# A gather order, a deferred up sum, a gate and a table load moved in the tail of a one-core Perceiver block

## The reference, cut to what matters

```python
x = x + xattn(_layernorm(x), ctx, ctx, w_q, w_k, w_v, w_o)      # 4 batches, 16 heads, 2048 keys
x = x + retention(_layernorm(x), W_Q, W_K, W_V, W_G, W_O, gn_weight, gn_bias)
    # ... Yn = (Y - mean) * rsqrt(var + EPS); out = G * sigmoid(G) * (Yn * gn_weight + gn_bias) @ W_O
x = x + fff_block(_layernorm(x), ...)

def _fff(x, nw, nb, w1, b1, w2, b2, act):       # used four times: q, k, v (relu) and f (gelu)
    node = 0
    for _ in range(8):
        logit = einsum('bsd,bsd->bs', x, nw[node]) + nb[node]
        node = 2 * node + 1 + (logit > 0)
    leaf = node - 255
    h = act(einsum('bsd,bsdl->bsl', x, w1[leaf]) + b1[leaf])    # 16 hidden values per token
    return einsum('bsl,bsld->bsd', h, w2[leaf]) + b2[leaf]

# fff_block: q, k, v = three trees of xn; y = xn + softmax(q k^T / sqrt(D)) v; return y + f(y)
```

## Time and profile before

| what | value |
|---|---|
| median of 3 runs | 668.21 us (666.90 to 668.83) |
| profiled execution, its own time | 667.87 us |
| its span, first to last instruction | 666.0 us |
| granted TensorE clock, mean | 0.987 |
| busy share PE / DVE / ACT / Pool | 93% / 68% / 59% / 40% |
| the same in the tail alone, 586 to 666 us: PE, DVE, ACT, Pool | 71%, 50%, 32%, 43% |

### The profile page before, as it was taken

One profiled execution on the slowest core, in us unless ns is written; L12 is line 12 of the kernel. 1 busy time (PEld: TensorE's weight loads), 2 busy tenths in 40 slices (PEclk: granted clock), 3 DMA queues, 4 the chain that ended last, 5 costly groups with the idle time before them and its releaser, 6 DMA issues.

```text
span 666.0 us, 10952 instructions
## 1 busy us (share of the span) xinstructions
PE 617.3 (93%) x4214; PEld 537.9 (81%) x4217; DVE 452.2 (68%) x800; ACT 391.7 (59%) x834; POOL 269.5 (40%) x259
## 2 busy tenths in 40 slices
PE   8899999999999999898999999899999999887486
PEld 4688888999998989787989889678989898774475
DVE  2566656778766777776777776786777777754644
ACT  3765556576655555668564855867556855730254
POOL 3210001131111106895252347886161439845632
PEclk9999999999999999999999999999999999998599
DMA  9810000020100007140030027120120035203903
GB/s 200 226 34 1 1 0 1 1 64 19 47 1 1 1 1 274 52 131 0 1 132 1 1 76 317 38 95 1 25 108 1 1 107 223 67 2 131 386 7 138
DMA packets 21403, 48.54 MB, mean 73 GB/s; under 512 B 1509, under 2 KB 14697, under 8 KB 17257
## 3 DMA queue, kind: packets, MB, share of 16 engines
q0 software_dynamic: 4608, 34.74, 13.9%
q1 hardware_dynamic: 16168, 12.85, 7.2%
q10 hardware_dynamic: 576, 0.26, 0.1%
HBM read 47.59 MB, written 0.26 MB: 72 GB/s over the span
## 4 chain that ended last, share of the span: by engine, by line
PE 64%; POOL 12%; DVE 10%; ACT 6%; DMA 3%; SPq 2%; issue 2%; POOLq 0%; DVEq 0%; ACTq 0%
PE ps_s L442 22%; PE ps_av L442 20%; PE ps_ring L710 13%; POOL leaf L1502 4%; PE ps_ring L442 4%; PE ps_m L442 4%; DVE pt_lo L1133 2%; POOL leaf L1506 2%; DVE chunk_max L1353 2%; ACT prob L1048 2%; ACT pt_hi L979 2%; POOL ct_lo L1471 2%; DVE hid L1194 1%; DMA stage<-ctx_rows_dram 1%; DMA leaf<-down_f_dram,idx 1%
## 5 line engine op out<-in xcount | busy, mean ns | idle before, releaser
L979 ACT CAST pt_hi<-ps_ring 128x512 fp32r<-128x512 f32 x256 | 144.4, 590 | 147.2 <-PE ps_ring L710 146.9
L1133 DVE TENSOR_TENSOR pt_lo<-ps_ring,pt_hi 128x512 fp32r<-128x512 f32 x256 | 170.0, 686 | 65.3 <-ACT pt_hi L979 65.3
L1048 ACT ACTIVATE prob<-ps_s,neg_max 128x1024 f32<-128x1024 f32 x128 | 141.7, 1114 | 27.9 <-DVE neg_max L1436 27.7
L710 PE MATMUL ps_ring<-ident,prob 128*128 128x128 f32 x1024 | 145.0, 274 | 12.9 <-DVE q_lo L1133 4.9
L1353 DVE TENSOR_REDUCE chunk_max<-ps_s 128x1 f32<-128x1024 f32 x128 | 150.5, 1215 | 4.1 <-PE ps_s L442 3.9
L442 PE MATMUL ps_av<-pt_hi,c_hi 128*128 128x256 f32 x512 | 151.2, 295 | 0.0
L710 PEld LDWEIGHTS ps_ring<-ident,prob 128*128 128x128 f32 x1024 | 116.8, 140 | 40.1 <-issue 19.7
L442 PE MATMUL ps_av<-pt_lo,c_hi 128*128 128x256 f32 x512 | 144.7, 283 | 0.0
L442 PE MATMUL ps_av<-pt_hi,c_lo 128*128 128x256 f32 x512 | 144.6, 283 | 0.0
L442 PE MATMUL ps_s<-ct_hi,q_hi 128*128 128x512 f32 x256 | 112.6, 440 | 3.1 <-ACT prob L1048 2.4
L442 PE MATMUL ps_s<-ct_hi,q_lo 128*128 128x512 f32 x256 | 101.8, 398 | 0.0
(11 more groups left out here) (277 smaller groups left out, 754.1 us busy)
## 6 DMA issues: line engine op xcount, KB each, us to landing
stage<-ctx_t_dram SPq DMA_DIRECT2D x16, 256.0 KB, 3.1
stage<-ctx_rows_dram SPq DMA_DIRECT2D x16, 256.0 KB, 3.2
leaf<-w_v_dram SPq DMA_DIRECT2D x1, 512.0 KB, 7.8
leaf<-w_o_dram SPq DMA_DIRECT2D x1, 512.0 KB, 10.0
dec<-decay_dram SPq DMA_DIRECT2D x1, 512.0 KB
nw<-node_w_dram SPq DMA_DIRECT2D x1, 510.0 KB
wsm<-w_small_dram SPq DMA_DIRECT2D x1, 448.0 KB
leaf<-wq_t_dram SPq DMA_DIRECT2D x1, 384.0 KB, 10.9
```

The costliest lines, as they stand in the source:

```text
L710: last = nc.tensor.transpose(o[:, i * P:(i + 1) * P], prob[:, n % 2, k:k + P], ident[:])
L979: nc.scalar.copy(pt_hi[:, pp, row:row + KPC, P * (n % 2):P * (n % 2 + 1)], ps_ring[:, i % 2, :].rearrange("p (k q) -> p k q", k=KPC)).then ...
L1048: nc.scalar.activation(prob[:, n % 2, 1024 * e:1024 * (e + 1)], ps_s[:, 1024 * e:1024 * (e + 1)], ACT.Exp, bias=neg_max[:, n:n + 1], accum ...
L1133: return nc.vector.tensor_tensor(o, a, b_, op)
```

## The change

No arithmetic is added or removed but for seven idle products that become four ahead of `gated_t`, with three new ones ahead of the third batch's f tree. The rest is a different order or a different engine:

- Gathers of the last batch: up q, down q, up k, up v, down k, down v becomes up q, up k, down q, down k, up v, down v. Pool's `weigh0` and `up2` move behind `up1` and `weigh1`.
- The third batch's up sum on DVE moves from behind the last `pick_f` to behind the last batch's softmax scaling (place 68 of the last batch), and no longer waits for the last cast of leaf numbers.
- All 16 down blocks of the third batch's f tree go to ACT (12 before, 4 on DVE).
- The last batch's gate: Pool only forms the root and signals `group_root`; the product and the sum run on DVE, behind the third batch's `pick_f`.
- Both halves of the last batch's masked queries on DVE; before, the second was Pool's.
- The gelu table load on ACT moves from ahead of the `y_t` copies to behind them.
- The third batch's `attv` on PE moves behind the last batch's `score1`.

```diff
 BEFORE_LAST_AT = {
-    ... ("PE", "attv"): 77.5, ...
+    ... ("PE", "attv"): 79, ...
-    ... ("ACT", "gelu"): 106,
-    ("ACT", "down3"): 107,
+    ... ("ACT", "gelu"): 105,
+    ("ACT", "down3"): 106,
-    ... ("DVE", "hid3"): 107,
+    ... ("DVE", "hid3"): 100,
-    ("DVE", "own3"): 108,
+    ("DVE", "own3"): 1000,
 LAST_AT = {
+    ("DVE", "gate"): 51, ("Pool", "mask_q"): 1000,
-    ... ("Pool", "weigh0"): 58, ("Pool", "weigh1"): 62, ("Pool", "up2"): 60, ...
+    ... ("Pool", "weigh0"): 60, ("Pool", "weigh1"): 62, ("Pool", "up2"): 63, ...
-    ("ACT", "load_gelu"): 70,
+    ("ACT", "load_gelu"): 72,
-WARM = {("gated_t", B - 1): 7, ("xf_t", B - 1): 12}
+WARM = {("logits_f", B - 2): 2, ("path_f", B - 2): 1, ("gated_t", B - 1): 4, ("xf_t", B - 1): 12}
 def shares(b, t):
-    return (0, 12, 4) if (b, t) == (B - 2, 3) else (LW, LW // 2, 0)
+    return (0, LW, 0) if (b, t) == (B - 2, 3) else (LW, LW // 2, 0)
 def leaf_sum(t, pieces=None):
-                        pe.wait_ge(S["own_ready"], 2)
+                        pe.wait_ge(S["own_ready"], 1)
 def third_sum():
-                pe.wait_ge(S["own_ready"], 1)
-                for l in range(shares(B - 2, 3)[1], LW):
-                    mm(o, ident[:], rows[:, D * l:D * (l + 1)], False, False)
 def hidden_layer(b, t):
                     dve.wait_ge(S["got_up3"], 16 * (b + 1))
-                    dve.wait_ge(S["idx_ready"], 4 * B)
 # DVE, "rope" of the last batch
                         masked_queries(nc.vector, 0).then_inc(S["qmask_last"], 1)
+                        masked_queries(nc.vector, 1).then_inc(S["qmask_ready"], 1)
 # DVE, new step
+                elif k == "gate":
+                    bc = rstd[:].rearrange("p (h o) -> p h o", o=1).to_broadcast([P, RH, RE])
+                    dve.wait_ge(S["group_root"], 1)
+                    dve.wait_ge(S["scaled"], b + 1)
+                    link(tt(groups(gated), groups(yc), bc, ALU.mult))
+                    dve.wait_ge(S["silu_ready"], b + 1)
+                    tt(gated, gated, shift, ALU.add).then_inc(S["gated_ready"], 1)
 # Pool, "gate"
                     pool.wait_ge(S["var_ready"], variances(b, 1))
+                    if last:
+                        root(0, RH, var[:]).then_inc(S["group_root"], 1)
+                        return
 # Pool, "gather_up01" of the last batch
                     gather(b, 0)
-                    pool.wait_ge(S["ring_filled"], RING[("T", HEADS - 1, CH - 1)] + 1)
-                    pool.wait_ge(S["ring_free"], BY_DVE[("X", HEADS + 3, 0)])
-                    gather_down(b, 0)
                     pool.wait_ge(S["picked"], 4 * b + 3)
                     nc.gpsimd.tensor_copy(idx[:, 1:3], chosen[:, 1:3]).then_inc(S["idx_ready"], 2)
                     pool.wait_ge(S["idx_ready"], 4 * b + 3)
                     gather_up(b, 1)
+                    pool.wait_ge(S["ring_filled"], RING[("T", HEADS - 1, CH - 1)] + 1)
+                    pool.wait_ge(S["ring_free"], BY_DVE[("X", HEADS + 3, 0)])
+                    gather_down(b, 0)
+                    gather_down(b, 1)
                     gather_up(b, 2)
-                    gather_down(b, 1)
                     gather_down(b, 2)
```

More of the change, by code:

```diff
@@ L62 @@
 BEFORE_LAST_AT = {
-    ("PE", "qk_t"): 72, ("PE", "att"): 73.5, ("PE", "v_half"): 73, ("PE", "v_rest"): 76, ("PE", "attp_t"): 76, ("PE", "attv"): 77.5, ("PE", "y_t"): 80,
+    ("PE", "qk_t"): 72, ("PE", "att"): 73.5, ("PE", "v_half"): 73, ("PE", "v_rest"): 76, ("PE", "attp_t"): 76, ("PE", "attv"): 79, ("PE", "y_t"): 80,
     ("PE", "logits_f"): 81, ("PE", "path_f"): 82,
-    ("ACT", "qk_t"): 73, ("ACT", "att"): 76, ("ACT", "attp_t"): 77, ("ACT", "v_sum_copy"): 78, ("ACT", "y_t"): 81, ("ACT", "gelu"): 106,
-    ("ACT", "down3"): 107,
-    ("DVE", "attmax"): 75, ("DVE", "y"): 80, ("DVE", "turns_f"): 82, ("DVE", "pick_f"): 83, ("DVE", "hid3"): 107,
+    ("ACT", "qk_t"): 73, ("ACT", "att"): 76, ("ACT", "attp_t"): 77, ("ACT", "v_sum_copy"): 78, ("ACT", "y_t"): 81, ("ACT", "gelu"): 105,
+    ("ACT", "down3"): 106,
+    ("DVE", "attmax"): 75, ("DVE", "y"): 80, ("DVE", "turns_f"): 82, ("DVE", "pick_f"): 83, ("DVE", "hid3"): 100,
     ("Pool", "res"): 82, ("Pool", "gather3"): 83, ("Pool", "up3"): 1000, ("Pool", "weigh3"): 1000, ("Pool", "fold3"): 1000,
@@ L88 @@
 LAST_AT = {
+    ("DVE", "gate"): 51, ("Pool", "mask_q"): 1000,
     ("PE", "vg"): 43, ("DVE", "silu"): 48, ("PE", "logits_v"): 54, ("PE", "path_v"): 55, ("DVE", "turns_v"): 55, ("DVE", "pick_v"): 56,
     ("Pool", "gather_up2"): 57, ("Pool", "gather_down01"): 56, ("Pool", "gather_down2"): 57,
-    ("Pool", "up1"): 59, ("Pool", "weigh0"): 58, ("Pool", "weigh1"): 62, ("Pool", "up2"): 60, ("Pool", "weigh2"): 66,
+    ("Pool", "up1"): 59, ("Pool", "weigh0"): 60, ("Pool", "weigh1"): 62, ("Pool", "up2"): 63, ("Pool", "weigh2"): 66,
     ("Pool", "up3"): 75, ("Pool", "weigh3"): 78,
@@ L332, in program @@
             q0_done q0_ready ct_split c_split s_done negmax_ready exp_done ring_filled ring_free
-            ring_taken block_ready own_ready third_blocks third_sum sum_done v_copied ap_scaled v_weighed v_summed roped root_ready gain_ready scaled ysq_ready wv_centred qmask_last hi_done av_done av_taken dve_link pool_link wv_turned wvt_ready wvo_done wvo_ready xn1_ready xn1t_done
+            ring_taken block_ready own_ready third_blocks third_sum sum_done v_copied ap_scaled v_weighed v_summed roped root_ready gain_ready scaled group_root ysq_ready wv_centred qmask_last hi_done av_done av_taken dve_link pool_link wv_turned wvt_ready wvo_done wvo_ready xn1_ready xn1t_done
             xn1t_ready gatedt_ready xft_ready qkt_ready apt_ready yt_ready qk_done qk_copied
@@ L1598, in rest @@
                     pool.wait_ge(S["qkx_ready"], b + 1)
[L1599 to L1603, removed]
+                    masked_queries(nc.gpsimd, 0)
+                    masked_queries(nc.gpsimd, 1).then_inc(S["qmask_ready"], 1)
                 elif k == "gain":
@@ L1607, in rest @@
                         pool.wait_ge(S["wv_centred"], 1)
-                    pool.wait_ge(S["qmask_last" if last else "qmask_ready"], 1 if last else b + 1)
+                    pool.wait_ge(S["qmask_ready"], b + 1)
                     link(nc.gpsimd.tensor_tensor(silu[:], gate, silu[:], ALU.mult))
```

## The result

The changed kernel takes 664.19 us (median of 7 runs, 661.91 to 666.11) against 668.21 for the kernel before (7 runs, 666.35 to 670.96): a ratio of 0.9944, 95% interval 0.9925 to 0.9962, that is 3.7 us less (2.5 to 5.0). The forecast was 664.6 in a range of 663.0 to 667.2.

What follows compares the result with a forecast made beforehand. Bound taken as the tail's chain of waits: idle products, PE's additions, table load, Pool's held issue, gathers. Terms -1.5 + 0.6 - 0.8 - 1.9 = -3.6 gave 664.6 us on the median of 668.21, range 663.0 to 667.2.

Steps and rivals of the forecast that it cites:

- Issue of f's up rows: Pool's gather issue in the tail: without DVE's product beside it, 1.06 us instead of 2.99, rows 1.9 us earlier.
- The reading from one row: Pool's 2.99 us issue ended 0.87 after DVE's product, an issue's own length: taken as Pool held while DVE runs.
- Table load: ACT's load ahead of the transposed y's copy: moved behind the copies, it leaves the path, -0.8 us.
- Gate stage: Last batch's gate: fewer idle products, `attv` off the path, less in Pool's queue; -1.5 us, bounds -1.0 and -1.9.
- The limit by Pool's queue: Gate stage: `root2` waits behind Pool's `res` and two f gathers, issued 1.0 earlier; the queue lets about 1.8 us through.
- Six gathers: New gather order: q's down rows third, PE's additions of q and k start later and end +0.6 us, -0.1 to +1.3.
- The same 5.0 us from PE's first product: PE's additions of q and k: clock assumed to rise 5.0 us after PE's first product at 626.87, at 631.9.
- The values of v: v's hidden values come some 0.8 us later, but v's blocks are taken up behind the copy at 636.8: stay covered.
- The up sum's new place: DVE's third-batch up sum behind the scaling ends at 644.0, as the f tree's comparison comes: 0, at most +0.3 us.
- the clock ahead of the trees: Rival: with four idle products the clock stays low and the twelve before `xf_t` end after `xf`; 666.5 us, chance 0.14.
- the issue was held by DVE: Its rival: Pool's 2.99 us issue has another cause and stays, sum -1.7, 666.5 us, chance 0.10.
- the clock came back in the additions: Its rival: clock stays low through the additions of k and v, costing 7.0 us; 671.6 us, chance 0.05.

## Why the prediction held, step by step

**Issue of f's up rows:** forecast -1.9, measured -1.95 in the profile. With that part alone it is -2.0 from the issue on, of which the cast behind DVE's own blocks gave back 0.4; with the product left in its place and one input in PSUM it is -1.8. The reading from one row (the issue ends one issue's length behind DVE's product) was right, and the PSUM run shows its cause.

**Table load:** forecast -0.8, measured -0.79 and -0.78.

**Gate stage:** forecast -1.5, measured -1.17 in the profiled pair and -0.97 in the second profile of the changed kernel, at the edge of its bounds. Between profiles whose clock did not fall at the gate it is -0.96 (17.97 to 17.01), and 0.75 of this is the gate on DVE. The term that was too large is the idle products: the prediction held the three new ones to lie in PE's waits. At the low clock the first two took 0.73 us of the chain, and the comparison of the third batch's f tree came 0.50 later than without them (7.36 against 6.86 after the first masked product; 7.08 before, so `attv` did give its 0.2). The clock then rose within the four, which took 1.27 and not 1.6. Without the three new ones the stage was no shorter (17.48), since the clock rose later there, 11.2 us after the first masked product against 9.1. The limit by Pool's queue that the prediction named was real: it is what holds the issue at 17.76 to 17.98 with the gate on Pool. By its own rows the queue lets 1.6 through and not 1.8 (608.79 - 1.0 against 609.43).

**Six gathers:** forecast +0.6, measured -0.35 in the profiled pair and about +0.1 in the means, which don't exclude 0.6. The late first addition was right: forecast 1.5 us after q's hidden values (627.3 - 625.81), measured 1.4 to 2.2, against 0.66. What failed in the account is a term at nothing: the wait for k's down rows, which the old order has and the new one hasn't. The prediction left it out, and in the profile of before it is only some 0.3; over six profiles it is 0.6. "The same 5.0 us from PE's first product" did not hold either (the rise came 2.9 to 4.7 us after the first added block in the new order), but with the rise where it was the later start still costs 0.5, so that step is not what took the 0.6 away. The values of v, which the prediction held to stay covered, came level with the scores' copy and cost 0.03.

**The up sum's new place:** forecast a tie, measured a tie (0.01 and 0.02 us between its end and the comparison in the two profiles of the changed kernel). It is hidden by nothing but PE's last additions of v: whatever shortens these will meet it.

**The rivals:** the clock ahead of the trees did not overrun `xf`; the issue was held by DVE; the clock came back in the additions in every profile. The sum, -3.6 by steps, measured -4.1 in the profiled pair and -3.7 by the ratio. That it came out so near is partly luck: the gate stage gave 0.3 to 0.5 less than forecast, and the gathers cost about 0.5 less.

## What to carry to other kernels

When a DMA issue on one engine is three times as long as its siblings, look at what another engine runs beside it and whether both inputs lie in SBUF; moving that work, or one input to PSUM, cost little and gave 1.6 to 2.0 us here. Idle products that are to keep a clock up are queued work: place them so that they end before what they stand ahead of, at the low clock, and look at the queue that becomes the next wait. When the clock's rise lies inside a stretch, don't price an edit from one profile of it: two orders whose first addition differs by 1.1 us came out 0.1 apart in the means of eleven, and it took a sum over each profile to see the two waits that cancel. And before an edit is given the credit for a shorter stage, look whether the clock fell there in both profiles.

## What the runs showed that was not expected

The clock's rise did not move with the start of the additions: in ten of eleven profiles it came 13.6 to 13.7 us after the fall, although PE's first added block lay 2.9 to 6.2 us before it. Thirteen idle products behind the landing of q's up rows brought it to 6.8 us after the fall in both kernels that had them, so earlier work does move it; what fixes the moment these runs don't show. And one and the same gather, that of q's up rows, landed from 5.8 to 8.6 us after its issue over thirteen profiles.
